# Cross-attention and expert kernel on one core: the product of probabilities and values written transposed, in groups of 32 columns, with the softmax sums beside it

## The reference

```python
qp = (q + pe) @ Wq.T + bq ; kp = (k + pe) @ Wk.T + bk ; vp = v @ Wv.T + bv
qh, kh, vh = (split_heads(qp), split_heads(kp), split_heads(vp))
scores = jnp.einsum('bhqd,bhkd->bhqk', qh, kh) * d_head ** (-0.5)
scores = scores - m.astype(scores.dtype) * NEG
attn = jax.nn.softmax(scores, axis=-1)
out = jnp.einsum('bhqk,bhkd->bhqd', attn, vh)
out = out.transpose(0, 2, 1, 3).reshape(b, l, d_model)
return out @ Wo.T + bo
```

## Time and profile before

| | us |
|---|---|
| median of 3 runs (769.43 to 773.44) | 770.99 |
| the profiled execution, its own time | 765.94 |
| span of its trace | 763.8 |
| TensorE busy in the span | 574.9 |
| VectorE busy | 443.1 |
| ScalarE busy | 407.7 |

### The profile page before, as it was taken

One profiled execution on the slowest core, in us unless ns is written; L12 is line 12 of the kernel. 1 busy time (PEld: TensorE's weight loads), 2 busy tenths in 40 slices (PEclk: granted clock), 3 DMA queues, 4 the chain that ended last, 5 costly groups with the idle time before them and its releaser, 6 DMA issues.

```text
span 763.8 us, 14153 instructions
## 1 busy us (share of the span) xinstructions
PE 574.9 (75%) x4326; PEld 405.7 (53%) x4326; DVE 443.1 (58%) x1706; ACT 407.7 (53%) x862; POOL 359.7 (47%) x438
## 2 busy tenths in 40 slices
PE   3499999889888988898898767483778866789800
PEld 1156666556455555555465446362667755679700
DVE  4267788778777877777785773251323322223374
ACT  2257988887787888688786655230322322224300
POOL 4122126644554564455435326647555555550075
PEclk9989999999999999999998987867898999989955
DMA  3363111221122122201111224324544444446498
GB/s 89 71 195 84 45 41 44 61 67 43 50 60 66 29 65 63 66 24 30 38 29 32 83 59 122 105 77 112 158 133 124 118 125 124 120 131 186 133 364 291
DMA packets 74458, 73.59 MB, mean 96 GB/s; under 512 B 22032, under 2 KB 61840, under 8 KB 74096
## 3 DMA queue, kind: packets, MB, share of 16 engines
q1 hardware_dynamic: 64160, 53.86, 26.8%
q0 software_dynamic: 8640, 18.37, 6.8%
q10 hardware_dynamic: 1584, 0.46, 0.2%
HBM read 44.99 MB, written 27.70 MB: 95 GB/s over the span
## 4 chain that ended last, share of the span: by engine, by line
PE 53%; ACT 14%; issue 13%; DVE 7%; another core or an unknown queue 4%; POOL 4%; SPq 2%; DMA 2%; ACTq 0%; POOLq 0%; DVEq 0%
PE bank L638 12%; PE bank L649 10%; PE bank L462 6%; PE bank L484 6%; DVE sm L890 3%; PE bank L466 3%; POOL gathered L1417 3%; PE bank L475 3%; PE bank L629 3%; ACT sm L717 2%; ACT pt L782 2%; ACT vx L709 2%; ACT rows L744 2%; PE bank L491 2%
## 5 line engine op out<-in xcount | busy, mean ns | idle before, releaser
L1354 POOL DMA_INDIRECT routed_rows<-rows,pos x128 | 125.2, 978 | 136.4 <-ACT rows L746 86.2
L1390 POOL DMA_INDIRECT expert_rows_by_token<-yb,token_row x118 | 113.2, 960 | 85.7 <-DVE token_row L1248 40.8
L638 PE MATMUL bank<-xbT,wi 128*128 128x256 f32 x312 | 97.1, 439 | 71.1 <-issue 70.4
L827 ACT ACTIVATE hb<-bank 128x512 f32<-128x512 f32 x78 | 46.6, 597 | 168.7 <-PE bank L638 77.4
L1254 DVE TENSOR_TENSOR yb<-bank,gate 128x256 f32<-128x256 f32 x78 | 33.1, 424 | 172.2 <-PE bank L649 107.2
L638 PEld LDWEIGHTS bank<-xbT,wi 128*128 128x128 f32 x312 | 59.6, 212 | 84.7 <-issue 77.0
L882 DVE TENSOR_REDUCE smax<-bank 128x8 f32<-128x512 f32 x128 | 82.2, 683 | 30.7 <-PE bank L466 25.4
L649 PE MATMUL bank<-wo,hb 128*128 x624 | 91.6, 295 | 0.0
L649 PEld LDWEIGHTS bank<-wo,hb 128*128 128x128 f32 x624 | 85.3, 212 | 0.1
L462 PE MATMUL bank<-kx,qT 64*64 64x512 f32 x512 | 74.6, 654 | 14.0 <-DMA kx<-kT 7.1
L890 DVE TENSOR_TENSOR sm<-bank,smax 128x512 f32<-128x512 f32 x128 | 81.9, 681 | 0.0
(11 more groups left out here) (135 smaller groups left out, 934.8 us busy)
## 6 DMA issues: line engine op xcount, KB each, us to landing
xb<-routed_rows SPq DMA_DIRECT2D x78, 138.0 KB
wi<-w_in SPq DMA_DIRECT2D x78, 128.0 KB
kx<-expert_rows_by_token SPq DMA_DIRECT2D x26, 256.0 KB
ctx_in<-ctx_t SPq DMA_DIRECT2D x16, 256.0 KB
x_all<-x SPq DMA_DIRECT2D x16, 256.0 KB
kx<-kT SPq DMA_DIRECT2D x256, 16.0 KB
out<-x_all SPq DMA_DIRECT2D x16, 256.0 KB
expert_rows<-yb SPq DMA_DIRECT2D x19, 128.0 KB, 2.1
```

The lines of the kernel that those rows point to most:

```text
L638: last = nc.tensor.matmul(UBK[b % 2][:, c * BLK:(c + 1) * BLK], wi[:, b % RX, c * P:(c + 1) * P], xbT[:, b % RH, :], start=True, stop=True)
L1354: nc.gpsimd.indirect_dma_start(out=rows_d, out_offset=bass.IndirectOffsetOnAxis(ap=pos[:, buf, k, u:u + 1], axis=0), in_=rows[:, buf, u, : ...
L1390: nc.gpsimd.indirect_dma_start(out=tok_d, out_offset=bass.IndirectOffsetOnAxis(ap=token_row[:, b % RY, u:u + 1], axis=0), in_=yb[:, b % RY ...
```

## The change

`vx` gets a layout in which two head pairs `2g` and `2g + 1` share a group `g` of 32 output rows. For each of the two batches `b` and each `j` in 0, 1, the stationary operand is a window of 32 columns, of which 16 hold values and 16 are zero; the moving operand is the 64 queries of that batch alone. The two `j` accumulate. Eight more matmuls with a constant stationary operand of 32 columns give the sums into the next 128 columns. `XB` then holds the result transposed (features by queries) in 128 columns, the sums in 128 more.

```diff
-                    for j in range(J):
-                        o = VM * (j % 2)
-                        last = nc.tensor.matmul(XB[o:o + VM, (j // 2) * P:(j // 2 + 1) * P], vx[:, u, j, :],
-                                                pt[:, j, :], start=True, stop=True)
+                    for j in range(2):
+                        for b in range(2):
+                            for g in range(J // 2):
+                                v = vx[:, u * (J // 2) + g, :, :].rearrange("p a c -> p (a c)")
+                                c = (2 * j + b) * VB
+                                nc.tensor.matmul(XB[g * VB:(g + 1) * VB, b * L:(b + 1) * L], v[:, c:c + VB],
+                                                 pt[:, 2 * g + j, b * L:(b + 1) * L], start=(j == 0 and b == 0),
+                                                 stop=False, skip_group_check=True)
+                    for j in range(2):
+                        for g in range(J // 2):
+                            last = nc.tensor.matmul(XB[g * VB:(g + 1) * VB, P:2 * P],
+                                                    ones_s[:, j * VB:(j + 1) * VB], pt[:, 2 * g + j, :],
+                                                    start=False, stop=(j == 1), skip_group_check=True)
                     last.then_inc(s_pv, 1)
 
                 def queries_to_rows(t):
                     pe.wait_ge(s_xev, t + 1)
-                    for c in range(4):
+                    for c in range(2):
                         last = nc.tensor.transpose(YB[:, c * P:(c + 1) * P], xo[:, c, :], ident[:, :])
                     last.then_inc(s_tq, 1)
...
-                            o = (2 * b + p) * DH
-                            last = nc.scalar.activation(dst[p * 64:p * 64 + 64, :, o:o + DH],
-                                                        src[b * 64:b * 64 + 64, :, p, :], ACT.Copy)
+                            o = b * VB + p * DH
+                            last = nc.scalar.activation(vx[p * 64:p * 64 + 64, :, :, o:o + DH],
+                                                        src[b * 64:b * 64 + 64, :, :, p, :], ACT.Copy)
...
-                        nc.scalar.activation(xo[:, :, :].rearrange("p c q -> p (c q)"), XB[:, :], ACT.Copy
+                        nc.scalar.activation(xo[:, :, :].rearrange("p c q -> p (c q)"), XB[:, 0:2 * P], ACT.Copy
                                              ).then_inc(s_xev, 1)
...
-                    y = YB[:, :].rearrange("r (j m) -> r j m", m=VM)
-                    nc.vector.reciprocal(rden[:, :, :], y[:, :, 4 * DH:4 * DH + 2]).then_inc(s_rden, 1)
+                    sums = YB[:, P:2 * P].rearrange("r (g m) -> r g m", m=VB)
+                    nc.vector.reciprocal(rden[:, :, :], sums[:, :, 0:4]).then_inc(s_rden, 1)
                     dve.wait_ge(s_rden, t + 1)
-                    for b in range(2):
-                        r = slice(b * 64, b * 64 + 64)
-                        last = nc.vector.tensor_tensor(
-                            on[r, :].rearrange("r (j p c) -> r j p c", p=2, c=DH),
-                            y[r, :, 2 * DH * b:2 * DH * (b + 1)].rearrange("r j (p c) -> r j p c", p=2),
-                            rden[r, :, :].unsqueeze(3).broadcast_to([64, J, 2, DH]), ALU.mult)
-                    last.then_inc(s_norm, 1)
+                    heads = rden[:, :, :].rearrange("r g m -> r (g m)")
+                    nc.vector.tensor_tensor(on[:, :].rearrange("r (h c) -> r h c", c=DH),
+                                            YB[:, 0:P].rearrange("r (h c) -> r h c", c=DH),
+                                            heads.unsqueeze(2).broadcast_to([P, H, DH]), ALU.mult).then_inc(s_norm, 1)
...
-                for u in range(U):
-                    last = nc.vector.tensor_copy(vx[:, u, :, :], ones_s[:, :].unsqueeze(1).broadcast_to([P, J, VM]))
-                last.then_inc(s_zero, 1)
+                nc.vector.memset(vx[:, :, :, :], 0.0).then_inc(s_zero, 1)
```

More of the change, by code:

```diff
@@ L31 @@
 EPS = 1e-5
-VM = 64
+VB = 32
 J = H // 2
@@ L95, in build @@
     spread_c = nc.inline_tensor((NEG_B * np.eye(P)).astype(np.float16), name="mask_spread")
-    ones_cols = np.zeros((P, VM), np.float32)
-    for p in range(2):
-        ones_cols[p * L:(p + 1) * L, 4 * DH + p] = 1.0
+    ones_cols = np.zeros((P, 2, VB), np.float32)
+    for j in range(2):
+        for p in range(2):
+            ones_cols[p * L:(p + 1) * L, j, 2 * j + p] = 1.0
+    ones_cols = ones_cols.reshape(P, 2 * VB)
     ones_c = nc.inline_tensor(ones_cols, name="value_ones")
@@ L140, in build @@
         causal = sb("causal_s", [P, L])
-        ones_s = sb("ones_s", [P, VM])
+        ones_s = sb("ones_s", [P, 2 * VB])
         wg1_s, bg1_s, wg2_s = sb("wg1_s", [D, G]), sb("bg1_s", [P, 1]), sb("wg2_s", [P, U, E])
@@ L164, in build @@
         kx = sb("kx", [P, 2, HH, U * P])
-        vx = sb("vx", [P, U, J, VM])
+        vx = sb("vx", [P, U * J // 2, 2, 2 * VB + 2 * DH])
         sm = sb("sm", [P, 2, H, L])
@@ L168, in build @@
         pt = sb("pt", [P, J, P])
-        xo = sb("xo", [P, 4, P])
-        rden = sb("rden", [P, J, 2])
+        xo = sb("xo", [P, 2, P])
+        rden = sb("rden", [P, J // 2, 4])
         on = sb("on", [P, D])
@@ L703, in v_evac @@
                     act.wait_ge(s_v, s + 1)
-                    src = W0[:, :].rearrange("r (uj p c) -> r uj p c", p=2, c=DH)
-                    dst = vx[:, :, :, :].rearrange("r u j m -> r (u j) m")
+                    src = W0[:, :].rearrange("r (g j p c) -> r g j p c", j=2, p=2, c=DH)
                     for b in range(2):
                         for p in range(2):
-                            o = (2 * b + p) * DH
-                            last = nc.scalar.activation(dst[p * 64:p * 64 + 64, :, o:o + DH],
-                                                        src[b * 64:b * 64 + 64, :, p, :], ACT.Copy)
+                            o = b * VB + p * DH
+                            last = nc.scalar.activation(vx[p * 64:p * 64 + 64, :, :, o:o + DH],
+                                                        src[b * 64:b * 64 + 64, :, :, p, :], ACT.Copy)
                     last.then_inc(s_vev, 1)
```

## The result

The changed kernel is slower: 816.75 us (813.51 to 821.16, 4 runs) against 771.61 us (769.43 to 773.44, 4 runs) for the kernel before, a ratio of 1.059 with the interval 1.054 to 1.064. The profiled execution took 816.22 us, its span is 814.4.

A forecast was written before the change was run, and what follows sets the result against it. No engine alone was taken as the bound, but a chain of waits across ScalarE, TensorE and VectorE, 25.73 us a step. Savings of 0.65 us over 16 steps, 10.4 us, took 770.99 to 761 us, range 755 to 774.

The forecast's parts named there:

- The terms of the chain: Savings in one step's chain of waits: `xo` 0.22 us twice and back-transposes 0.21 once, 0.65 us a step.
- the product: VectorE's `normalise`: two products of 289 ns become one near 291; 0.29 us saved a tile, counted at nothing.
- the memset: Setting of `vx` at the start: 2.17 us instead of 1.43, ahead of idle VectorE, so no cost.
- The back-transposes: TensorE's four back-transposes a tile become two, saving 0.21 us, counted once in a step's chain.
- `values` at the rate of rows 6: TensorE's 48 records of `values` run four side by side as L530's do: 0.88 us, same as now.
- Rival 4: In `values`, only two of four column groups overlap: 1.76 us, 0.88 longer; 789 us, up to 817; chance 0.10.
- rival 2: Each `values` record costs 25 ns whatever it streams: 1.20 us, nothing gained, 771 us (768 to 774); chance 0.17.
- the unnamed wait: Last 1.76 us of a step's chain, ending on something the profile does not name; left unchanged in the sum.
- with the 16 steps alike: The sum took the 0.65 us saving for every attention step: 16 x 0.65 = 10.4 us.
- rival 3: The 1.76 us wait at the chain's end swallows two of three savings: 3.5 us left, 767.5 us; chance 0.11.
- if all pieces are as said but the step is still 25.5, the unnamed wait has grown: Sign in the changed profile that the wait ate the gain; the step was forecast at 25.1 us instead of 25.73.
- The clock: TensorE's granted clock, 1.00 in both stretches, might drop with less work; the lower level would double the slots.

The follow-up runs named there:

- before_late: Kernel before the change, with all indirect scatters of GpSimd issued after the attention: step 23.90 us against 25.82; total 888.53 us, no measure because of the moved work.
- after_late: Changed kernel, with all indirect scatters of GpSimd issued after the attention: step 23.31 us against 30.73; total 876.37 us, no measure because of the moved work.
- before_tiny: Kernel before the change, plus 32 small fp16 matmuls of zeros behind `values` of each tile: 840.59 us (one run), step 31.46 us.
- after_k1_late: Changed kernel with four of the eight indirect transfers a step left in the attention, the others issued after it: step 25.23 us, total no measure.

## Why the prediction was wrong

- *The terms of the chain were right.* `xo` 385 ns for 379 forecast, the product 291 ns once a tile, the memset 2.19 us for 2.17 and hidden. The back-transposes' 128 records (L502) are busy 27.2 us for 40.8. Together they are worth 0.59 us a step where nothing disturbs them (before_late, after_late), 0.65 predicted.
- *`values` at the rate of rows 6 was right.* 1.09 us a tile for 48 records, with 0.47 us from the first record of 64 columns to the first of 128 (280.57 to 281.04; 0.44 forecast). Rival 4 (groups in turn, 1.76 us) and rival 2 (25 ns a record, 1.20 us of starts) are both refuted by the tile at 280.57: L489's 32 records are done 0.65 us after the first starts and each lasts 0.22, so 31 intervals take 0.43 us, 14 ns each. The floor of 25 ns of the Trainium skill (TensorE: Matmul & The Clock Gate, Back-to-back issue gap) does not hold for matmuls in different column groups; the trace decides. The largest number of rival 4, 817 us, is the measured time by chance: it stood for `values` of 1.76 us on all four tiles, and at `u` = 3 they take 1.09.
- *The step that failed is the one on the unnamed wait.* The sum left it as it stood, "with the 16 steps alike", and rival 3 let it take gains at most: 3.5 us left, 767.5. The 16 steps aren't alike: the first three have no transfers. The prediction's sign "if all pieces are as said but the step is still 25.5, the unnamed wait has grown" named the right place, but only as something that eats the gain: the step went to 30.73, 4.9 us over that of the kernel before. The wait was TensorE's own: it ends when TensorE's records and signals get through beside GpSimd's indirect transfers (without these it is gone, before_late), and it grows with what the change triples, the records (before_tiny). I had counted `values` by the columns that it streams and never asked what its 48 records share with other engines.
- *The evidence was in the trace of before.* `xo` started 2.24 us after the last record of `values` at `u` = 0, and 0.05 us after it at `u` = 3 (its records end at 288.35, and it starts at 288.40); four indirect transfers lay beside the first and none beside the second; and none of the first twelve tiles, which have no transfers beside them, waited over 0.32 us.
- *The clock* was named as another way to fail. It fell from 1.00 to 0.96 in the stretch from 220 to 260 us, and from 0.83 to 0.81 in the part behind the attention, which is 7.5 us longer. It is not the cause of the stalls: in the stretch from 286.5 to 292 us, which holds those of the tile shown, it is 1.00, and after_k1_late has its stalls at 1.00 throughout the attention. From 60 to 100 us, where no indirect transfer is, it stays at 1.00, and so it does over the whole attention in the late kernels: it falls where TensorE stalls. What it adds has an upper bound. The eleven steps from tile 16 to tile 60, before and after:

```profile
136.31:431.44 295.13, 256.81 (x2217) 161.04 (x2217) 227.87 (x855) 228.95 (x482) 146.35 (x193) 0.98 0.19 47
132.95:474.92 341.97, 285.85 (x3537) 162.12 (x3537) 211.09 (x810) 221.46 (x482) 146.47 (x194) 0.94 0.16 41
```

If everything in a stretch went at TensorE's pace, the lower clock would have cost 0.02 x 295 = 5.9 us before and 0.06 x 342 = 20.5 after, 1.9 us a step. So at most some 15 of the 46.8 us are the clock's, an estimate from these rows, and over 30 are the stalls' own.

How the loss grows with records: `values` to `xo` at `u` = 0 is 3.39, 4.96, 5.02, 5.09 us for 16, 24, 32, 48 records, beside 1.42 without transfers. (With 8 it is 1.42 too, but there the delay falls on what comes behind.) It levels off near 5 us, about the length of the four transfers together (285.72 to 290.50, 4.78 us). So a cost of the kind "so much for a record" is right only in the middle. That the time in which indirect transfers run is the upper bound fits these numbers, but no run tests it. From 24 to 32 records the tiles at `u` = 1 and 2 go on to grow (1.85 and 1.79 us to 3.26 and 3.59); from 32 to 48 the four waits together hardly do (12.59 and 12.90).

What stays open is the path that the two share. Every execution timed here was recorded like the profiled one, so whether the recording has a part in it (each TensorE record is one more thing to write out) can't be told from these runs. The Trainium skill (NOTIFIC — the notification-queue block, Overflow: three behaviours, one of which stalls the engine) says that the block's inner pipeline holds its producers back rather than lose a record; no run here shows whether that is what happens.

## What to carry to other kernels

Count TensorE's instructions, not only its columns: splitting the matmuls was free here where no indirect transfer of GpSimd ran beside them, and dear where one did, so put the two in different stretches, or keep the matmuls few. When a chain of waits has a piece without a name, look at what every other engine does in just that stretch, and at the same instruction in a step without it, before leaving it as a constant in a sum. And when a change's terms are small (0.65 us a step), a stall of 1.8 us in the same chain that is not understood is the largest risk in it.

## What the runs showed of the hardware that was not expected

- Matmuls in four column groups start 14 ns apart on average over 32 records; 48 records in 1.09 us.
- Beside an indirect transfer of GpSimd (0.97 us each) TensorE gets through one to five records in each 0.73 us or so once it is behind; when it is not, its records look undisturbed and its signals reach ScalarE and VectorE about 3 us late (3.8 and 2.8). Plain transfers of GpSimd or SyncE with the same bytes do nothing of the kind.
- Eight indirect transfers a step cost 7.4 us with 48 records a tile, 6.9 with 32, 1.9 with 16, the lower clock beside them included; four cost 1.9 with 48, at a clock of 1.00.
